# Batch 0's first two levels of a chunked recurrence moved among the last projections, with its token sums in 128-row products

## The reference

```python
xn = _layernorm(x, gamma, beta)
w = jax.nn.sigmoid(jnp.einsum('btc,cd->btd', jnp.einsum('btc,cd->btd', xn, Wx), Ww) + bw)
k = jnp.einsum('btc,cd->btd', xn, Wk)
v = jnp.einsum('btc,cd->btd', xn, Wv)
r = jax.nn.sigmoid(jnp.einsum('btc,cd->btd', xn, Wr))
...
def step(state, inp):                      # 4 heads of 64 channels
    k_t, v_t, w_t, r_t = inp
    kv = k_t[..., :, None] * v_t[..., None, :]
    state = (1.0 - w_t)[..., :, None] * state + kv
    y_t = jnp.einsum('bhi,bhij->bhj', r_t, state)
    return (state, y_t)
```

## Time and profile before

| | |
|---|---|
| median of three runs | 886.52 us (879.02 to 890.49) |
| the profiled execution | 887.58 us, span of its instructions 885.7 us |
| TensorE busy | 787.7 us, 89% of the span |
| VectorE busy | 696.1 us, 79% |
| ScalarE busy | 522.2 us, 59% |
| GpSimd busy | 365.1 us, 41% |
| last products of the projections begin | 609.15 us into the span |
| first product of the mixing begins | 612.43 us |
| level 6 of the recurrence begins on VectorE | 661.12 us |

### The profile page before, as it was taken

One profiled execution on the slowest core, in us unless ns is written; L12 is line 12 of the kernel. 1 busy time (PEld: TensorE's weight loads), 2 busy tenths in 40 slices (PEclk: granted clock), 3 DMA queues, 4 the chain that ended last, 5 costly groups with the idle time before them and its releaser, 6 DMA issues. The chain is left out here.

```text
span 885.7 us, 17904 instructions
## 1 busy us (share of the span) xinstructions
PE 787.7 (89%) x6593; PEld 509.2 (57%) x6593; DVE 696.1 (79%) x1101; ACT 522.2 (59%) x957; POOL 365.1 (41%) x296
## 2 busy tenths in 40 slices
PE   3999999999999999999999998996657588999996
PEld 2863333333333333333388887985647486999875
DVE  5789999999899999994167666669999385666586
ACT  4420788887688888887854335444576343666542
POOL 5430344446553564468210000105775670344340
PEclk9985899999699999999999999998687798999999
DMA  6597023222022223100057000001006222344352
GB/s 234 196 215 261 2 53 68 59 57 53 12 55 60 60 53 61 21 16 16 14 176 151 1 1 13 1 1 57 5 12 244 86 81 43 111 129 129 107 173 72
DMA packets 59510, 69.97 MB, mean 79 GB/s; under 512 B 24768, under 2 KB 46400, under 8 KB 59040
## 3 DMA queue, kind: packets, MB, share of 16 engines
q1 hardware_dynamic: 55272, 58.30, 24.5%
q0 software_dynamic: 3408, 9.38, 3.1%
q10 hardware_dynamic: 744, 1.15, 0.4%
HBM read 40.07 MB, written 26.62 MB: 75 GB/s over the span
## 5 line engine op out<-in xcount | busy, mean ns | idle before, releaser
L681 ACT ACTIVATE probs_t<-psum 128x512 f32<-128x512 f32 x512 | 271.7, 601 | 100.9 <-PE psum L781 99.1
L695 DVE TENSOR_REDUCE row_max<-psum 128x1 f32<-128x1024 f32 x256 | 298.1, 1214 | 11.0 <-PE psum L765 10.7
L622 POOL TENSOR_TENSOR lut_sum<-lut_sum,lut_tmp 128x1080 f32<-128x1080 f32 x60 | 151.9, 2532 | 164.8 <-DVE lut_tmp L720 164.1
L765 PE MATMUL psum<-KS,QS 48*128 48x512 f32 x512 | 191.3, 477 | 18.8 <-DVE row_max L695 17.8
L781 PE MATMUL psum<-QS,KS 50*128 50x512 f32 x512 | 196.0, 474 | 1.4 <-ACT probs_t L681 1.4
L781 PEld LDWEIGHTS psum<-QS,KS 50*128 50x128 f32 x512 | 84.0, 191 | 136.6 <-ACT probs_t L681 128.6
L793 PE MATMUL psum<-probs_t,VS 128*32 128x512 f32 x1024 | 140.5, 622 | 1.0
L765 PEld LDWEIGHTS psum<-KS,QS 48*128 48x128 f32 x512 | 83.2, 202 | 74.8 <-DVE row_max L695 69.5
L2312 POOL DMA_INDIRECT y_rows<-y_slot,ids x39 | 37.3, 958 | 68.0 <-ACT y_slot L2376 67.7
L720 DVE TENSOR_SCALAR lut_tmp<-lut_idx,lut 128x1080 f32<-128x1080 int32 x60 | 48.7, 813 | 10.2 <-POOL lut_sum L622 10.2
L1178 POOL TENSOR_TENSOR rstd<-var_eps,minus_half 128x4 f32<-128x4 f32 x8 | 8.4, 1044 | 100.3 <-DVE var_eps L1173 100.3
(11 more groups left out here) (312 smaller groups left out, 1790.0 us busy)
## 6 DMA issues: line engine op xcount, KB each, us to landing
KS<-k_rows SPq DMA_DIRECT2D x31, 192.0 KB, 4.6
QS<-q_rows SPq DMA_DIRECT2D x31, 192.0 KB, 4.9
x_rows<-zero_rows SPq DMA_DIRECT2D x1, 4992.0 KB, 17.8
x_slot<-x_rows SPq DMA_DIRECT2D x39, 128.0 KB
m_raw<-experts_w SPq DMA_DIRECT2D x2, 2432.0 KB, 12.0
q_rows<-part SPq DMA_DIRECT2D x8, 512.0 KB, 8.7
y_token<-y_rows SPq DMA_DIRECT2D x8, 512.0 KB, 7.6
x_tok<-x SPq DMA_DIRECT2D x4, 512.0 KB, 7.5
```

What stands on the lines that cost most here:

```text
L622: nc.gpsimd.tensor_tensor(wsum[:, c % 2, :], wsum[:, c % 2, :], wtmp[:, slot % 2, :], ALU.add).then_inc(lut_add, 1)
L681: nc.scalar.activation(pt[:, k % NPT, :], ring(k)[:], ACT.Exp, scale=float(E) ** -0.5).then_inc(p_ready, 1)
L695: nc.vector.tensor_reduce(mx[:, n % 2, col:col + 1], m.psum[:, 2 * (k % 2):2 * (k % 2) + 2, :], AX_XY, ALU.max).then_inc(max_done, 1)
L765: mm = nc.tensor.matmul(MX[k % 2][h][:], QS[n % NQK][rows(g, NROW), st * P:(st + 1) * P], KS[n % NQK][rows(g, NROW), h * BLK:(h + 1) * BLK ...
```

## The change

It has three parts.

1. The token products hold 128 tokens each, not 32: 8 per group and level, not 32.
2. Groups 0 and 1 (batch 0) get their token products, their scaling of r and the taking of their sums in the projections' block. On TensorE group 0's products stand after the fourth item of token block 3, group 1's after the seventh. The tables `masks` and `diag` are loaded, and `heads` is set, earlier for it.
3. ScalarE takes all k and v of token block 3, and the v of token block 2, in VectorE's place.

```diff
-    def taken_by(kind):
-        return "act" if kind in "wr" else "dve"
+    def taken_by(k):
+        tb, kind = k // NIT, ITEMS[k % NIT][0]
+        return "act" if kind in "wr" or tb == NB - 1 or tb == NB - 2 and kind == "v" else "dve"
...
+    SMALL_BANK = [(0, 0, 1, 0), (7, 256, 7, 256 + NS), (4, 0, 5, 0), (6, 0, 7, 0)]
...
+    def tokens_weights(pe, l, g):
+        pe.wait_ge(q_done, 2 * g + l + 1)
+        out = small_bank(l, g).rearrange("p (h c) -> p h c", h=NH)
+        for c in range(NC):
+            mm = nc.tensor.matmul(out[:, :, c], Q[g][:, l, c * CH:(c + 1) * CH], m.heads[:], start=True, stop=True)
+        mm.then_inc(m.lev_ps, 1)
...
+    def take_tokens(dve, g):
+        w0, w1 = (small_bank(l, g).unsqueeze(2).broadcast_to([P, NS, QB]) for l in range(2))
+        dve.wait_ge(m.lev_ps, 2 * g + 2)
+        nc.vector.tensor_tensor(m.AD[g][:], w0, ...
...
-            for g, i in ((0, K0), (1, K1)):
-                m.multiply(dve, 0, g)
-                m.scale_r(dve, 0, g)
-                take(dve, 3 * NIT + i, 3)
-                m.multiply(dve, 1, g)
-            for i in (V0, V1):
-                take(dve, 3 * NIT + i, 3)
+            def token_products(g):
+                m.multiply(dve, 0, g)
+                m.scale_r(dve, 0, g)
+                m.multiply(dve, 1, g)
+            token_products(0)
             take(dve, 2 * NIT + K1, 2)
+            for step in range(1, 12):
+                place(step)
+            token_products(1)
+            m.scale_r(dve, 1, 0)
+            m.take_tokens(dve, 0)
             for step in range(12, NIDX):
                 place(step)
+            m.scale_r(dve, 1, 1)
+            m.take_tokens(dve, 1)
...
-            project(3, 0, NIT)
+            project(3, 0, 4)
+            pe.wait_ge(m.heads_ready, 1 + NH)
+            pe.wait_ge(yf_ready, NB * KC)
+            for l in range(2):
+                m.tokens_weights(pe, l, 0)
+            project(3, 4, 7)
+            pe.wait_ge(idx_done, 7)
+            for l in range(2):
+                m.tokens_weights(pe, l, 1)
+            project(3, 7, NIT)
...
-            for c in range(NC):
-                out = bank[2 * g + l][:, 0:NS].rearrange("p (h c) -> p h c", h=NH)[:, :, c]
-                for q in range(4):
-                    t = c * CH + q * QB
-                    mm = nc.tensor.matmul(out[QB * q:QB * (q + 1), :], Q[g][:, l, t:t + QB], heads[:],
-                                          start=True, stop=True)
...
-        for g in range(NCH):
+        for g in range(KC, NCH):
             for l in range(2):
-                tokens_weights(l, g)
+                m.tokens_weights(pe, l, g)
```

More of the change, by code:

```diff
@@ L1225, in time_mix_scales @@
     m.q_done, m.odd_zero, m.r_done, m.k_done, m.tot_done = q_done, odd_zero, r_done, k_done, tot_done
+    m.lev_take, m.mask_in, m.heads_ready = sem("lev_take"), sem("mask_in"), sem("heads_ready")
+    m.AD = [at(f"AD{g}", [P, NS, QB], F32, m.p3 + NCH * NS * CH * 4 + g * NS * QB * 4) for g in range(NCH)]
+    b = m.tot_end + 2 * NC * P * 4 + 2 * NC * LD * 4
+    m.masks = at("masks", [P, SMALL + 1, QB], I32, b); b += (SMALL + 1) * QB * 4
+    m.diag = at("diag", [P, QB], F32, b); b += QB * 4
+    m.heads = at("heads", [P, NH], F32, b); b += 32
@@ new lines, in time_mix_scales, with small_bank, r_at, load_masks @@
+    m.heads_end = b
+    SMALL_BANK = [(0, 0, 1, 0), (7, 256, 7, 256 + NS), (4, 0, 5, 0), (6, 0, 7, 0)]
+    def small_bank(l, g):
+        first = SMALL_BANK[g][2 * l + 1]
+        return m.bank[SMALL_BANK[g][2 * l]][:, first:first + NS]
+    def r_at(l, g):
+        return (1, 2, 5, 6, 3, 4, 7, 8)[l * NCH + g] if l <= 1 else l * NCH + g + 1
+    def load_masks(sp, a):
+        sp.dma_start(m.masks[:], a["masks"]).then_inc(m.mask_in, 16)
+        sp.dma_start(m.diag[:], a["diag"]).then_inc(m.mask_in, 16)
@@ new lines, in set_heads @@
+    def set_heads(pool):
+        nc.gpsimd.memset(m.heads[:], 0.0).then_inc(m.heads_ready, 1)
+        pool.wait_ge(m.heads_ready, 1)
+        for h in range(NH):
+            nc.gpsimd.memset(m.heads[h * LD:(h + 1) * LD, h:h + 1], 1.0).then_inc(m.heads_ready, 1)
+            pool.wait_ge(m.heads_ready, 2 + h)
+    def tokens_weights(pe, l, g):
[4 more added lines that the diff above has]
+        mm.then_inc(m.lev_ps, 1)
@@ L1406, in time_mix_in_stage @@
     RING = 5
-    def taken_by(kind):
-        return "act" if kind in "wr" else "dve"
+    def taken_by(k):
+        tb, kind = k // NIT, ITEMS[k % NIT][0]
+        return "act" if kind in "wr" or tb == NB - 1 or tb == NB - 2 and kind == "v" else "dve"
     def order(k):
-        who = taken_by(ITEMS[k % NIT][0])
-        per = sum(taken_by(x[0]) == who for x in ITEMS)
-        return k // NIT * per + sum(taken_by(x[0]) == who for x in ITEMS[:k % NIT + 1])
+        return sum(taken_by(j) == taken_by(k) for j in range(k + 1))
     def rbank(k):
@@ L1511, in _ @@
             out_b(3)
-            for g in range(2, NB):
-                for i in (W0, R0, W1, R1):
-                    take(act, g * NIT + i, g)
+            for k in range(2 * NIT, NB * NIT):
+                if taken_by(k) == "act":
+                    take(act, k, k // NIT)
         @block.vector
@@ L1808, in time_mix_stage @@
     m.R2 = R2
-    AD = [at(f"AD{g}", [P, NS, QB], F32, b + g * NS * QB * 4) for g in range(NCH)]
+    AD = m.AD
     Q, TOT, b = m.Q, m.TOT, m.tot_end
@@ L1813, in time_mix_stage @@
     yl = at("ty_l", [P, KC, T], F32R, m.base + KC * T * 4)
[L1814 to L1817, removed]
+    masks = m.masks
+    assert b + (SMALL + 2) * QB * 4 + 32 == m.heads_end and m.heads_end <= m.rt_at, b
     raw_in, shared_in = sem("e_w_in"), sem("e_shared_in")
     m.w_hi, m.w_lo = sem("w_hi"), sem("w_lo")
-    heads_ready, r2_zero, r2_in = sem("heads_ready"), sem("r2_zero"), sem("r2_in")
+    r2_zero, r2_in = sem("r2_zero"), sem("r2_in")
     q_done, r_done, k_done, tot_done, lev_ps, r_back = m.q_done, m.r_done, m.k_done, m.tot_done, m.lev_ps, m.r_back
```

73 lines of the change are left out of this document (30 added, 43 removed).

## The result

Over 20 runs each, the changed kernel took 893.9 us (886.7 to 903.95) and the kernel before 887.05 us (879.02 to 894.87). The ratio is 1.0082, with a 95% interval of 1.0058 to 1.0106: the change costs 5 to 9 us. That is no difference by a bound of 2%, but it is clear of noise, and slower. The ratio leaves out one run of the changed kernel, 903.95 us, in the slower state that some runs of any kernel show.

A forecast was written before the change was run, and what follows sets the result against it. Ahead of level 2 VectorE's work was taken as the bound, with TensorE meeting it. Block end +7.1 us, less 4.4 of taking, less 0.2 of waits, gave +2.5: 886.5 to 889.0 us, with 0.95 on 868.8 to 904.2.

The forecast's parts named there:

- A wide record costs 0.116 us at full clock: Token sums on TensorE: one record with 128 stationary columns takes 0.116 us, so 32 records, one group, take 3.7 us.
- TensorE has no hole among the projections: Token block 3 on TensorE: the sums of groups 0 and 1 are extra work and move its end by +7.1 us.
- A: Stretch from VectorE's fifth key copy to its first product of the mixing; the forecast had the mixing begin 7.1 us later.
- The second rival: Projections: the clock falls at group 0's sums, half clock adds 13 us to the forecast, 902 us; chance 0.08.
- I take a rise within the sums: Mixing, sums of groups 2 and 3: 26 records at half clock, 38 at full, ending at 630.9 us.
- The first rival: Mixing: the clock stays low through the sums of groups 2 and 3; level 2 +7.5 us, 894 us; chance 0.2.
- VectorE's 4.4 us leave the mixing: Taking groups 0 and 1 (2 x 2.22 us) moves from the mixing to where VectorE waits for TensorE in the projections.
- B: Stretch from VectorE's first product of the mixing to its first scaling for level 2; forecast 4.4 us shorter.
- TensorE's pauses lie beside VectorE's work: Mixing ahead of level 2: VectorE decides, so TensorE's pauses of 4.25, 1.57 and 2.12 us are covered by its work.
- C: Stretch from VectorE's first scaling for level 2 to level 6; forecast unchanged except for 0.2 us less.
- levels 2 to 5 in less than 30 us: Stated sign that the prediction is wrong: levels 2 to 5 after the mixing's sums take less than 30 us.
- The other signs of being wrong: Wide records much under 0.11 us; clock not full at 604 to 617; VectorE waiting over 1 us for TensorE at 628-633.

## Why the prediction came out as it did

The range and the sign were right; the likeliest case was not the one that came. The forecast was +2.5 us, and the ratio makes it +7.3. That the range held says little, for 2% either way takes in no change at all and every one of the cases, from 885 to 902 us. By stages, with the second profiles of both kernels, the forecast's terms came so: the way to the mixing +8.1 us (+7.1 forecast), the mixing up to level 2 -0.6 (-4.4), levels 2 to 5 -0.4 (-0.2). The gain that was to pay for most of the cost did not come. Point by point:

- **A wide record costs 0.116 us at full clock: right.** Measured 3.63 us for 32 where the clock held, 3.7 predicted from the logits' row. The bound at half clock, 7.4 us a group, was 6.9 measured (13.82 for two groups).
- **TensorE has no hole among the projections, so the block's end moves by 7.1 us: right at full clock.** A was 29.1 in the kernels whose clock held, 22.6 + 6.5: two sums of 3.63 us, less the 0.7 us that ScalarE's takes gave. With the change's own long runs it was 8.1 and 11.9 more. The second rival ("the clock falls within the projections") was on that account partly true: I gave it 0.08 and priced it at +13 for the whole stretch, and it came for a part of the stretch, at 1.6 and 5.5 us over 29.1.
- **"I take a rise within the sums": the step that failed.** I took the clock's return at the end of the pauses in the earlier trace rows as TensorE's reward for being busy. The sums of groups 2 and 3 kept TensorE busy without a pause for 13.8 us at half clock, in both profiles, and 128 such records did for 25.7 us, all but the first 2 at half clock. So VectorE waited 3.61 us, and the mixing took 17.03 us up to level 2 where 13.3 was forecast. The first rival had this mechanism: 64 records at half clock, 894 us. It predicted level 2 at 18.1 us after the jump; 17.03 was measured, and 893.9 us for the whole. The two totals agree partly by luck: the rival's sum lacks the loss in the projections (1.6 and 5.5 us), and it has the mixing 1.1 us too long.
- **VectorE's 4.4 us leave the mixing: right, and hidden.** With 32-row products B is 4.9 us shorter. With wide ones VectorE waits 3.61 us for them and the gain is 0.6 to 0.7. No version had the wide sums of groups 2 and 3 at full clock throughout, so the forecast's own case was never seen.
- **TensorE's pauses lie beside VectorE's work: right ahead of level 2, nearly right behind it.** Ahead of it VectorE worked from 612.01 to 629.75 without a wait, and only where its work was 1.4 us less (the 32-row products with the sums back in the mixing) did it wait 1.16 us behind the pauses. In levels 2 to 5 of the profile that I worked from, VectorE waited 1.82 us for TensorE; I had named 0.85 of that. It is the 1.5 us by which this profile's C (31.37) stands above the second one's (29.90). In the twelve profiles of other versions C is 29.44 to 30.30, with pauses of 4.4 to 10.0 us. I called "levels 2 to 5 in less than 30 us" a sign of being wrong; it was the baseline's first profile that was slow, and that is why the change's profile seemed to give something back there.
- **The other signs of being wrong** named the right places: the clock between 604 and 617 was not full, and VectorE's wait for TensorE was above 1 us (3.61), though at 640 to 644 and not at 628 to 633.
- **ScalarE's copies are worth nothing: right within the noise**, 0.9989 (0.9963 to 1.0016), with 0.7 us by the stages.

What stays open is the exact condition under which the clock falls in the projections. Long runs of wide products lost it in the three profiles with two moving columns (once only after the run had ended), short runs kept it in two, long runs with 64 moving columns kept it in one.

## What to carry to other kernels

Fewer, larger products are not cheaper when the stationary side is what takes the time: merging four products of 32 columns, each into its own strip, into one of 128 made TensorE's time 2.9 times as long (3.63 against 1.27 us) to save instructions that nobody waited for. That the four overlap because they lie in different strips was not tested, for no version put narrow products into one strip; what the runs show is the price of either form. Before work is put between dense products, ask whether the engine has a hole there at all, and whether the work itself keeps the clock; if it must go there, short runs kept the clock here (29.1 us in place of 30.7 and 34.6 up to the mixing). And take a second profile of the baseline, on another chip too, before explaining a stall by the chain of waits: here "issue" was a quarter of the chain in one execution, and its pauses were nearly absent from levels 2 to 5 in the other.

## What the runs showed that I had not expected

- TensorE can be busy in every row of the trace and have half the clock throughout: 13.8 us of wide products in the change and over 20 us in the kernel with these products alone, without a pause and without a rise of the granted clock from 0.50.
- The pauses of about 2 us after each 127 or 128 records of small products are not a property of the program alone. In two executions of the same kernel they came to 12.1 and 1.0 us before the level-2 to level-5 products; in the state update they were absent on two chips (four profiles) and 6.6 to 9.5 us in the ten other profiles. What makes them differ stays open.
- Widening the moving side from 2 to 64 columns behind 128 float32 stationary ones changed the pace by 0.05 us in 32 records.
